# One scores pass instead of two in a fused transformer block: maxima as the bias of the exponential, and P turned by DMA transposes

## The reference

```python
x = x + 0.5 * ffn(layernorm(x))
x = x + attn(layernorm(x))
x = x + 0.5 * ffn(layernorm(x))

def attn(x):                                   # 16 query heads, 4 key/value heads, head width 16
    q, k, v = projections of x, plus biases    # q, k: RMS norm per head, rope, q times a gain
    s = (q / 4) @ k.T                          # per head, 256 x 256
    s = where(key <= query, s, -inf)           # causal
    return softmax(s) @ v  ->  @ Wo.T + bo

def ffn(x):                                    # 8 experts of width 512
    w = top_p_weights(softmax(x @ router_w.T), 0.9)
    return sum over e of w[:, e] * ((silu(x @ gate[e].T) * (x @ up[e].T)) @ down[e].T)
```

## Time and profile before

| | |
|---|---|
| median of 3 runs | 1144.59 us (1144.28 to 1146.37) |
| profiled execution, its own time | 1144.43 us |
| its span in the trace | 1142.2 us |
| busy: PE, DVE, POOL, ACT | 97%, 71%, 59%, 45% of the span |
| granted clock of PE | full in all slices |

### The profile page before, as it was taken

The page is one execution under the profiler, slowest core; times in us unless marked ns, Lnnn a source line. Parts: engine busy times, 40 slices in busy tenths (PEclk is TensorE's granted clock), DMA queues, the critical chain, the costliest instruction groups (busy, mean ns, idle before and its releaser), DMA issues.

```text
span 1142.2 us, 21578 instructions
## 1 busy us (share of the span) xinstructions
PE 1112.3 (97%) x7689; PEld 660.5 (58%) x7689; DVE 809.9 (71%) x1993; ACT 518.2 (45%) x868; POOL 668.2 (59%) x737
## 2 busy tenths in 40 slices
PE   5899999999999999999999999999999999999998
PEld 2456556565555555565565655555656566665665
DVE  7878887679788777778777778768767455554443
ACT  4544544433454554445445454454454544333332
POOL 4545444368488677667767768768655464333222
PEclk9999999999999999999999999999999999999999
DMA  5411110001110110011111011021110000000000
GB/s 185 133 56 56 63 62 2 9 11 42 29 33 15 29 29 19 19 29 24 16 29 24 15 29 24 16 46 25 25 24 20 10 11 1 11 19 1 1 1 20
DMA packets 73273, 34.66 MB, mean 30 GB/s; under 512 B 65360, under 2 KB 69968, under 8 KB 73168
## 3 DMA queue, kind: packets, MB, share of 16 engines
q1 hardware_dynamic: 73168, 33.27, 11.4%
HBM read 15.70 MB, written 2.10 MB: 16 GB/s over the span
## 4 chain that ended last, share of the span: by engine, by line
PE 63%; DVE 5%; POOL 4%; issue 1%; ACT 1%; DVEq 0%; ACTq 0%; POOLq 0%
PE YB L358 19%; PE G L339 19%; PE U L339 18%; PE S L492 1%; PE S L469 1%; PE S L507 1%; DVE S L930 1%; PE S L423 1%; POOL HS L1061 1%; POOL room L1157 1%; DVE TS L685 1%; DVE TS L690 1%; POOL RR L1117 1%; PE S L449 1%; DVE X L706 1%
## 5 line engine op out<-in xcount | busy, mean ns | idle before, releaser
L1061 POOL TENSOR_TENSOR HS<-TS,HS 128x512 f16<-128x512 f32 x256 | 301.1, 1176 | 379.4 <-ACT HS L560 378.4
L358 PE MATMUL YB<-W,HS 128*128 128x256 f16 x3036 | 374.4, 273 | 9.7 <-DVE X L706 6.3
L339 PE MATMUL G<-XS,W 128*128 128x512 f16 x1536 | 375.0, 380 | 1.7 <-ACT XS L585 1.7
L339 PE MATMUL U<-XS,W 128*128 128x512 f16 x1536 | 373.5, 379 | 1.1 <-DVE W L791 1.1
L358 PEld LDWEIGHTS YB<-W,HS 128*128 128x128 f16 x3036 | 290.0, 98 | 92.3 <-DVE X L706 13.4
L685 DVE SCALAR_TENSOR_TENSOR TS<-TS,G 128x512 f32<-128x512 f32 x256 | 175.3, 685 | 223.3 <-ACT TS L553 223.1
L560 ACT ACTIVATE HS<-TS 128x512 f16<-128x512 f32 x256 | 161.4, 631 | 311.7 <-DVE TS L690 311.5
L553 ACT ACTIVATE TS<-G,TSC 128x512 f32<-128x512 f32 x256 | 175.5, 686 | 216.5 <-PE G L339 210.2
L339 PEld LDWEIGHTS U<-XS,W 128*128 128x128 f16 x1536 | 150.3, 98 | 182.9 <-DVE W L791 1.6
L339 PEld LDWEIGHTS G<-XS,W 128*128 128x128 f16 x1536 | 146.9, 98 | 135.3 <-issue 2.0
L690 DVE SCALAR_TENSOR_TENSOR TS<-TS,U 128x512 f32<-128x512 f32 x256 | 176.0, 688 | 28.7 <-DVE TS L685 1.8
(11 more groups left out here) (167 smaller groups left out, 712.5 us busy)
## 6 DMA issues: line engine op xcount, KB each, us to landing
room<-in_gate SPq DMA_DIRECT2D x4, 512.0 KB, 3.2
room<-in_up SPq DMA_DIRECT2D x4, 512.0 KB, 3.2
room<-in_down SPq DMA_DIRECT2D x4, 512.0 KB, 3.6
QKT<-in_gate SPq DMA_DIRECT2D x4, 512.0 KB, 3.3
QKT<-in_up SPq DMA_DIRECT2D x4, 512.0 KB, 3.6
QKT<-in_down SPq DMA_DIRECT2D x4, 512.0 KB, 4.5
out_y<-X SPq DMA_DIRECT2D x16, 128.0 KB, 1.8
X<-in_x SPq DMA_DIRECT2D x3, 512.0 KB, 6.2
```

The source lines that it names most:

```text
L339: mm = eng.matmul(bank[:, :], W[:, e, wl, jj, kk * I + m * P:kk * I + (m + 1) * P], flat(XS16[:, b % 2, xl, kk, :, :], 'cq'), start=q == 0 ...
L358: mm = eng.matmul(out, HS[:, j % 2, hl, kk, m * P:(m + 1) * P], W[:, e, wl, 2, kk * D:(kk + 1) * D], start=kk + hl + wl == 0, stop=kk == K ...
L1061: eng.tensor_tensor(HS[:, j % 2, 1, m, :], TS[:, k % 3, :], HS[:, j % 2, 0, m, :], ALU.subtract).then_inc(L['g_lo'].sem, 1)
```

## The change

The second pass, its second transposes and the masking on POOL go. The scores of the first pass (now `pe_scores`, in 48 rounds: two for an even tile, four for an odd one) are scaled by minus 1/4 and a power of two, masked, and left in PSUM by DVE, which also takes the minima of each row; ACT raises them from there with scale -1 and the row's minimum as bias. P has queries on the partitions then, and the product with V needs keys there: both fp16 halves of P (PHL) are turned by two DMA transposes of 128x1024 a round (`sp_pt`) into PT. The first two tiles' layer norm is turned by DMA too, where PE did it. Slots are laid out anew: `s` minus 126, modulo 36, is called r in this document, and with it rounds begin at r = 2, 8, 14, 20, 26, 32.

```diff
+PER = 6
+BATCH = 6 * PER
+FIRST = 126
+ROUND = [FIRST + 2 + PER * i for i in range(NR)]
+ROUNDS = [(2 * b + (r > 1), r - 2 if r > 1 else r) for b in range(B) for r in range(6)]
+def by_tile(even, odd):
+    return [FIRST + BATCH * (t // 2) + (odd if t % 2 else even) for t in range(NT)]
...
+Q_STEP = {'rb1': 2, 'sq': 2, 'rb0': 2, 'rr': 3, 'r': 4, 'qn': 5, 'v': 5, 'qh': 6, 'ql': 6, 't': 7}
+I_STEP = {'ma': 1, 'mb': 2, 'ea': 2, 'eb': 3, 'ha': 3, 'hb': 4, 'la': 4, 'lb': 5, 'ta': 5, 'tb': 6, 'pv': 8, 'o': 9}
...
+ATP, QKVP, OUTP = (by_tile(-17, -5), by_tile(-12, 0), by_tile(18, 42))
 ATT = [s - 4 for s in ATP]
...
         def pe_scores(eng, i, s):
+            t, j = ROUNDS[i]
...
+            heads, keys = (4, 1) if t % 2 == 0 else (2, 2)
+            for q in range(heads):
+                kv, c = (2 * j + q // 2, 4 * j + q) if t % 2 == 0 else (j, 2 * j + q)
+                for h, bank in ((0, S0), (1, S1)):
+                    mm = eng.matmul(bank[:, q * keys * P:(q + 1) * keys * P], QTT[rows(h), t % 2, c, :], KTT[rows(h), t // 2 % 2, 0:keys, kv, :], start=q == 0, stop=q == heads - 1, skip_group_check=True, tile_position=(64 * h, 0))
...
         def pe_pv(eng, i, s):
...
+            p_turned(eng, i, 0)
+            p_turned(eng, i, 1)
+            heads, keys = (4, 1) if t % 2 == 0 else (2, 2)
+            for q in range(heads):
+                for h in range(2):
...
+                    for kt in range(keys):
+                        for hl in range(2):
+                            mm = eng.matmul(o, PT[i % 2][:, h, hl * G + q * keys + kt, :], VS[:, t // 2 % 3, kt, kv, :], start=kt + hl == 0, stop=kt == keys - 1 and hl == 1)
...
+        def act_exp(eng, i, h):
+            eng.wait_ge(*L['v_mp'].at(i, 'ab'[h]))
...
+            heads, width = (4, P) if t % 2 == 0 else (2, 2 * P)
+            for q in range(heads):
+                a = eng.activation(P32[:, h, q * width:(q + 1) * width], (S0, S1)[h][:, q * width:(q + 1) * width], ACT.Exp, bias=MXN[:, i % 2, h, q:q + 1], scale=-1.0)
...
+        def act_ph(eng, i, h):
+            eng.wait_ge(*L['a_e'].at(i, 'ab'[h]))
+            p_turned(eng, i - 2, h)
+            eng.activation(PHL[:, i % 2, h, 0, :], P32[:, h, :], ACT.Copy).then_inc(L['a_ph'].sem, 1)
...
+        def dve_max(eng, i, h):
...
+            if t % 2 == 0:
+                x = bank[:, :].rearrange('p (g k) -> p g k', g=G)
+                eng.scalar_tensor_tensor(x, x, NESC[:, 0:1], MB[:, 1, :].unsqueeze(1).broadcast_to([P, G, P]), ALU.mult, ALU.subtract).then_inc(lane.sem, 1)
+                eng.tensor_reduce(MXN[:, i % 2, h, :], x, AX.X, ALU.min).then_inc(lane.sem, 1)
+            else:
+                for q in range(2):
+                    eng.tensor_tensor_reduce(x, x, flat(MB[:, :, :], 'ak'), NESC[:, 0:1], 3.0e38, ALU.add, ALU.min, MXN[:, i % 2, h, q:q + 1]).then_inc(lane.sem, 1)
...
-        def pe_max(eng, n, s):
-        def pe_atp(eng, t, s):
-        def act_ac(eng, t):
-        def dve_mm(eng, t):
-        def pool_qz(eng, t):
-        def pool_mask(eng, i, c):
-        def sp_q2(eng, t):
...
+        def pool_pl(eng, i, h):
+            eng.wait_ge(*L['a_ph'].at(i, 'ab'[h]))
+            eng.tensor_tensor(PHL[:, i % 2, h, 1, :], P32[:, h, :], PHL[:, i % 2, h, 0, :], ALU.subtract).then_inc(L['g_pl'].sem, 1)
...
+        def sp_pt(eng, i, h):
...
+            eng.wait_ge(*L['a_ph'].at(i, 'ab'[h]))
+            eng.wait_ge(*L['g_pl'].at(i, 'ab'[h]))
+            eng.dma_start(PT[i % 2][:, h, :, :], flat(PHL[:, i % 2, h, :, :], 'sk'), transpose=True).then_inc(s_pt[i % 2][h], 16)
 
         def sp_slot(eng, s):
+            for h in range(2):
+                for i in due(ROUND, s, I_STEP['t' + 'ab'[h]]):
+                    sp_pt(eng, i, h)
+            for t in due(ATP, s):
+                sp_atp(eng, t)
+            for t in due(QKVP, s, Q_STEP['t']):
                 sp_qt(eng, t)
                 sp_kt(eng, t)
             for f in due(FTP[2 * BT:], s):
                 sp_ftp(eng, f + 2 * BT)
```

More of the change, by code:

```diff
@@ L52, with last_round @@
 PREP = [-99, 0, 8, 24, 36, 47, 58, 72, 83]
[L53 to L74, removed]
+PER = 6
[5 more added lines that the diff above has]
+    return [FIRST + BATCH * (t // 2) + (odd if t % 2 else even) for t in range(NT)]
+def last_round(t):
+    return 6 * (t // 2) + (5 if t % 2 else 1)
 FTP0 = (3, 3, 6, 6)
 FIRST_FTP = (99, 102, 104, 109, 152, 152, 161, 161)
-FTP_LATER, ROUTE_LATER = (22, 25)
-ROUTE_FIRST = (3, 11, 112, 162)
+FTP_SOON, FTP_LATER, FTP_LAST, ROUTE_LATER = ((66, 68), (62, 64), (30, 51), 67)
+ROUTE_FIRST = (3, 11, 112, 174)
 A_STEP = {'ax': 3, 'xl': 3, 'bo': 6}
-Q_STEP = {'rb1': 2, 'sq': 2, 'rb0': 2, 'rr': 3, 'r': 4, 'qn': 5, 'qz': 4, 'v': 5, 'qh': 6, 'ql': 6}
-I_STEP = {'eb': 1, 'ea': 1, 'ma': 2, 'ec': 2, 'hb': 3, 'mc': 3, 'ha': 4, 'lb': 4, 'hc': 5, 'la': 4, 'lc': 5, 'pv': 7, 'o': 8}
+Q_STEP = {'rb1': 2, 'sq': 2, 'rb0': 2, 'rr': 3, 'r': 4, 'qn': 5, 'v': 5, 'qh': 6, 'ql': 6, 't': 7}
+I_STEP = {'ma': 1, 'mb': 2, 'ea': 2, 'eb': 3, 'ha': 3, 'hb': 4, 'la': 4, 'lb': 5, 'ta': 5, 'tb': 6, 'pv': 8, 'o': 9}
 R_STEP = {'r1': 1, 'ex': 1, 'r2': 1, 'r2b': 3, 'rank': 3, 'r3': 5}
@@ L318, in s2_read @@
             eng.wait_ge(*L['a_fc'].at(f, 'xs'))
-            pv_read(eng, s, (3,))
             if before(ROUTE, s) >= 3:
                 eng.wait_ge(*L['v_ls'].at(before(ROUTE, s), 'ls'))
-        def pv_read(eng, s, places):
-            i = max((i for i in range(NI) if i % 4 in places and ITEM[i] + I_STEP['pv'] < s), default=-1)
-            eng.wait_ge(*L['v_pv'].at(i, 'rd'))
         def pe_gu(eng, k):
@@ L522, in pe_slot @@
                 pe_wb(eng, e)
-            for i in due(ITEM, s):
+            for i in due(ROUND, s):
                 pe_scores(eng, i, s)
-            for i in due(ITEM, s, I_STEP['pv']):
+            for i in due(ROUND, s, I_STEP['pv']):
                 pe_pv(eng, i, s)
@@ L983, in dve_slot @@
                 dve_y(eng, (s - 10) // 2)
-            for n in due(MAXS, s, 1):
-                dve_max(eng, n)
-            for n in due(MAXS, s, MM_STEP):
-                if n in MAXN:
-                    dve_mm(eng, MAXN.index(n))
-            for i in due(ITEM, s, I_STEP['o']):
+            for h in range(2):
+                for i in due(ROUND, s, I_STEP['m' + 'ab'[h]]):
+                    dve_max(eng, i, h)
+            for i in due(ROUND, s, I_STEP['o']):
                 dve_pv(eng, i)
@@ L1238, in sp_atp, with qkt_raw, sp_qt @@
             eng.dma_start(XTA[:, :, :, :].rearrange('p h k q -> p (h k) q'), flat(XA16[:, :, :], 'hw'), transpose=True).then_inc(s_at, 16)
-        def qkt_freed(eng, t):
+        def qkt_raw(eng):
+            eng.wait_ge(*L['v_lo'].at(E - 1, 'lo1'))
+            eng.wait_ge(*L['g_w'].at(E - 1, 'lo2'))
+        def sp_qt(eng, t):
+            if t < 2:
+                qkt_raw(eng)
+            else:
+                eng.wait_ge(*L['p_sc'].at(last_round(t - 2), 'b'))
+            eng.wait_ge(*L['v_ql'].at(t, 'qlo'))
+            eng.dma_start(QTT[:, t % 2, :, :], flat(QS[:, :, :, :], 'hsc'), transpose=True).then_inc(s_qt, 16)
@@ L1254, in sp_kt @@
[L1254 to L1268 removed]
+                qkt_raw(eng)
+            else:
+                eng.wait_ge(*L['p_sc'].at(last_round(t // 2 * 2 - 3), 'b'))
@@ L1269, in sp_slot @@
+        def sp_slot(eng, s):
+            for h in range(2):
+                for i in due(ROUND, s, I_STEP['t' + 'ab'[h]]):
[3 more added lines that the diff above has]
+            for t in due(QKVP, s, Q_STEP['t']):
                 sp_qt(eng, t)
-            for t in due(KTP, s):
                 sp_kt(eng, t)
```

290 lines of the change are left out of this document (86 added, 204 removed), and 4 rows, old and new, of the table later.

## The result

| | before | after |
|---|---|---|
| median, same chip | 1144.69 us (1144.28 to 1146.37) | 1175.44 us (1173.48 to 1178.27) |
| profiled execution, its span | 1144.43, 1142.2 us | 1177.16, 1175.4 us |
| mean granted clock of PE | 1.0 | 0.981 |

The ratio is 1.0268 (95% interval 1.024 to 1.0296): 30.8 us slower. The forecast was 1150, the range 1128 to 1162. So the sign was right, and the time lies 13 us above the range.

The account below looks back on a forecast made before the run. The prediction took PE's issue queue as the bound: 1144.4 - 20.5 - 0.6 (work leaving PE) + 31 (new waits) = 1154.3, less 4 of old waits 1150.3, said as 1150. The range was 1128 to 1162.

Parts of the forecast that it names:

- PE's queue 21.1 us shorter: On PE, the second pass's 32 items (20.5 us) and eight transposes of the first two tiles (0.6 us) leave the queue.
- Costs of the moved operations: ACT's exponentials take 92 us at most, and DVE's even-round scaling and reduction 43 us in 16 rounds, both covered.
- The new wait: PE waits before the product with V at r = 34 for P's transposes: 4.4 us in seven turns, 31 us.
- the sign that the prediction named for itself: Wrong if PE's waits before V sum to under 25 us, spread over all rounds, or are on DVE.
- The first failed step: In the attention stretch, 4 of the 6.1 us in which PE stood vanish, as POOL has 40.7 us less.
- The second failed step: On PE before V at r = 34, each of seven waits costs just its length, 4.4 us, 31 us in all.
- The covered case: Rival: P's transposes are covered, so PE has no new wait: 1144.4 - 21.1 - 4 = 1119; chance 0.22.
- DVE adds more: Rival: DVE at r = 1 to 6 adds 12 us (1162), slow landings 10 (1160), both 1172; chance 0.16.
- The rule on issuing early: By the skill's rule, two slots between issue and wait cover each transpose of P: new wait nothing, time 1119.

Follow-up runs that it names:

- POOL's order: The kernel after, with the layer norm's small power (`pool_a_rs`) put behind the long power (`pool_rr`) in POOL's slot: 1164.62 us, ratio 1.0174 to the kernel before.
- SP's order alone: The kernel after, with SP's three foreign transposes due one slot later, behind P's second one: 1138.79 us, ratio 0.9948 to the kernel before.
- the best version: The kernel after with SP's three foreign transposes one slot later, odd tiles' layer norm two slots earlier, and four fused DVE instructions per even round's half: 1134.22 us.
- The two last experiments: Kernel after, foreign transposes one slot later, odd layer norm two earlier; then even rounds' mask and scale cut to 128 columns (1134.39 us), or four fused instructions (1134.22 us).
- SP's order and the layer norm four slots earlier: The kernel after with SP's three foreign transposes one slot later and the odd tiles' layer norm four slots earlier: 1136.66 us, ratio 0.9934 to the kernel before.
- the filled version: The kernel after, with PE multiplying 30 times into unread PSUM columns before the wait on P in six of seven turns: 1166.02 us, ratio 1.0189.
- SP's order and the earlier layer norm: The kernel after with SP's three foreign transposes one slot later and the odd tiles' layer norm two slots earlier: 1136.38 us, ratio 0.9933 to the kernel before.

## Why the prediction was wrong

- **PE's queue 21.1 us shorter: right.** Span less excess fell from 1122.8 to 1101.6, and for the eight experiments whose excess is given it is 1101.3 to 1102.4, so 20.4 to 21.5 us less.
- **Costs of the moved operations: right**, 90 for 92 us on ACT, 46 for 43 us on DVE. DVE as a whole was not: its new work was to be nearly paid by what goes, and it was busy 836.2 us after and 809.9 before, 26 more. Nor was it all hidden, as 10 us less of it gave back 2.2 us.
- **The new wait: right in place, cause and chain, too large in size.** It stood in seven turns, in r = 34, behind three foreign issues on SP's queue. In four of them it was 3.9 to 4.3 us, in two 3.2, in one 1.1: 23.6 us in place of 31. A turn is less because PE already came late, from the next point. By the sign that the prediction named for itself, waits before V of under 25 us in all, it had failed here: they sum to 24.0. The transposes landed in 3.2 us at the median, not in 2.8.
- **The first failed step, "I expect 4 to vanish, as POOL has 40.7 us less": wrong in sign.** Other waits of PE in the stretch rose from 7.9 to 8.7 + 13.4 = 22.1. The 13.4 are the down product at r = 31, on the same crowded slots. The prediction followed the lists there for P's chain only, not for the down product, whose `dve_y` stands behind `dve_qn`, and that behind POOL's long power (DVE's 0.56 us of waiting for it in the turn shown). That is not all of it: with POOL's order changed `dve_qn` waits no longer, and the down product stands 1.1 us all the same, behind the scaling that waits and takes longer (above). With the waits for P, it is 37.0 us in the seven turns, against 31. The sum has 7.9 less 4, 3.9 us, for the other waits: 18.2 too little, its largest miss.
- **The second failed step: a wait was priced as its length.** The sum took each stand at 4.4 us, and then PE at full speed. But behind each of the seven stands of 2.9 us and more in that stretch (six for P, one for DVE) PE's groups took up to twice their time, with a granted clock of 0.50 over 5.8 us in the turn shown: 16.5 us in all. Either failed step by itself takes the forecast above its range, to 1168.5 and to 1166.8; the waits for P, 7.4 us too large in the sum, hide a part of both. The forecast's 1150.3 with the three measured corrections, 23.6 - 31 for the waits for P, + 16.5 for the clock, and 22.1 - 3.9 for the others, is 1177.6; the profiled execution took 1177.2.
- **The rivals.** The covered case was what SP's order alone comes to: 1139, not 1119, since the other waits rose where 4 us less were expected. "DVE adds more" had the right engine and nearly the right size, some 10 of the 13.4 us for 12, but at r = 31 and not at r = 1 to 6; its 1162 to 1172 came nearest to the time, without the clock.
- **The rule on issuing early.** The Trainium skill (DMA: Bandwidth & Descriptors, Rules for kernel authors) wants the issue early and the wait late. The transposes were due two and three slots ahead, and PE still waited 24.0 us for them: due early is not issued early where an in-order queue has three issues of 1.33 us in front. Once it was issued in time, the rule held (0.5 us of waits in all).

What is still open: PE's waits in the best version are 30.1 us where before had 19.4, some 10 us more, in the attention stretch. The two last experiments took 10 and 13 us of DVE's work away and got some 2 back; what the rest hangs on was not tested, and POOL's long power was not taken away by itself. These waits hold half of the change's gain: 9.8 us came out of 21.1.

## What to carry over

Cut the work that leaves the bounding engine, then walk through every in-order queue that the new dependency crosses, DMA issue queues first; the first thing to try is the order of issues, as two shifted lines made 36.7 us here. Price a stand of the matrix engine by its length and by the slow groups that rows show behind one like it, and follow every consumer that meets in the crowded slots, not only the one that is new. When a stall moves, look one engine further on before you move another helper.

## What the runs showed of the hardware

**The clock behind a stand.** In the kernel after, 2.7 us were lost behind a stand of 3.9 us and 1.6 behind one of 3.2. Between 2.3 and 3 us it went either way. In the version with POOL's order a stand of 2.4 us was followed by a down product of 2.29 and a gate of 1.99 us (for 1.31 and 1.30), and with SP's order and the layer norm four slots earlier one of 2.35 by a down product of 2.53; but in the one with the layer norm alone two slots earlier a stand of 2.45 was followed by nothing, and so was one of 2.9 for DVE in the filled version, behind which the clock had fallen in the kernel after. In the stretch with attention, behind those under 2.3 us there was none in any run, and none where matmuls filled the stand. (At the start of the program, where PE waits every few us, the clock fell in most runs behind waits of 1.1 and 1.3 us.) So near this length the same kernel can pay or not: the six runs of the layer norm alone are 1145.2 and 1145.5 us at a mean granted clock of 0.999 and 1148.1 to 1150.1 at 0.996 and 0.997.

**What POOL does beside it sets the price of a DVE instruction.** The layer norm's scaling (128x256 fp32) took 401 ns at best and 1236 ns at worst; moved two slots, its median went from 475 to 1002 ns with no change to itself. The instructions of that tile in the kernel after (minimum, median and maximum in ns, first and last start):

```profile
L797 DVE TENSOR_SCALAR XNA<-X,MVA,RSA x16: 401/475/1236, 237.8 to 871.4; 128x256 f32<-128x256 f32 x16
```

The same in the version with SP's order and the earlier layer norm:

```profile
L797 DVE TENSOR_SCALAR XNA<-X,MVA,RSA x16: 539/1002/1246, 237.6 to 829.5; 128x256 f32<-128x256 f32 x16
```

The timelines tell which price comes when. In the turn shown of the kernel after it runs inside POOL's long power (696.64, 3.54 us) and is not slowed:

```profile
697.21 0.41 DVE L797 TENSOR_SCALAR XNA<-X,MVA,RSA 128x256 f32<-128x256 f32 x1
```

With POOL's order changed it starts 0.07 us behind a remainder of 128x512 (690.61, 1.16 us) and takes 1.24 (690.68, above). So it is in all sequences: 0.40 to 0.42 us inside the long power, 1.23 to 1.25 right behind the start of a remainder, and 0.71 to 0.77 behind one that began 0.54 to 0.59 earlier, which is the rest of the remainder and some 0.15. It is the kind of POOL's instruction that counts, and not that POOL is busy. The extra 26 us of DVE have a part in this: of the rounding of the keys' remainder (128x128, 16 times) an instruction took 787 ns on average after and 314 before.

So moving an instruction in time changes its price, by more than some moves win. The Trainium skill (SBUF — State Buffer, Who interferes with whom) has it that only the ports that VectorE and GpSimd share cause contention, and that one blocks the other for its whole instruction. The rows beside the remainders agree with it: DVE's instruction ends 0.15 us behind POOL's each time. Those inside the long power don't: POOL had begun 0.6 us earlier and went on for 3 us, and DVE's instruction took its 0.41 us all the same.
